# The product that updates the recurrent state, issued as 64x64 tiles instead of 64x128 tiles

## The reference, cut to what matters

```python
def step(state, inp):
    q_i, k_i, v_i, g_i, dec_i, kcd_i = inp
    attn = einsum('bhcd,bhed->bhce', q_i, k_i) * dec_i
    v_new = v_i - einsum('bhcd,bhde->bhce', kcd_i, state)
    out_i = einsum(q_i * exp(g_i), state) + einsum(attn, v_new)
    state = state * exp(g_last) + einsum('bhcd,bhce->bhde', k_i * exp(g_last - g_i), v_new)
```

## Time and profile before

| | |
|---|---|
| runs shown | 2787.59, 2787.88, 2792.42 us, median 2787.88 |
| the profiled execution's own time | 2787.02 us |
| its span | 2785.1 us |
| TensorE (matmul) busy | 2496.7 us, 90% |
| TensorE (weight load) busy | 1718.8 us, 62% |
| VectorE, ScalarE, GpSimd busy | 1660.4, 1492.5, 1802.1 us |
| TensorE's granted clock, mean | 0.982 of full speed |
| L548, the state product | 1792 matmul records, 162.8 us busy |

### The profile page before, as it was taken

One profiled execution on the slowest core, in us unless ns is written; L12 is line 12 of the kernel. 1 busy time (PEld: TensorE's weight loads), 2 busy tenths in 40 slices (PEclk: granted clock), 3 DMA queues, 4 the chain that ended last, 5 costly groups with the idle time before them and its releaser, 6 DMA issues.

```text
span 2785.1 us, 104069 instructions
## 1 busy us (share of the span) xinstructions
PE 2496.7 (90%) x41680; PEld 1718.8 (62%) x41680; DVE 1660.4 (60%) x2967; ACT 1492.5 (54%) x3206; POOL 1802.1 (65%) x1829
## 2 busy tenths in 40 slices
PE   3599999989999998999999899999899999998799
PEld 1366666666666666666666566666666666666444
DVE  5466666666666666666666566666566666665322
ACT  1456566555556566555556566555565566554211
POOL 0576667787666666787666667787666667787100
PEclk8799999999999999999999999999999999998899
DMA  3111011111111011111111011011110111110200
GB/s 96 35 35 31 16 31 39 30 34 33 35 35 31 17 30 40 28 35 33 35 35 31 17 31 39 28 35 33 36 35 16 32 31 39 27 35 2 58 22 16
DMA packets 71100, 90.28 MB, mean 32 GB/s; under 512 B 16720, under 2 KB 39376, under 8 KB 70480
## 3 DMA queue, kind: packets, MB, share of 16 engines
q1 hardware_dynamic: 70608, 83.40, 11.7%
HBM read 78.30 MB, written 5.08 MB: 30 GB/s over the span
## 4 chain that ended last, share of the span: by engine, by line
PE 68%; DVE 20%; issue 6%; DVEq 1%; ACT 1%; DMA 0%; POOLq 0%; ACTq 0%; SPq 0%; POOL 0%
PE ps_two L406 9%; PE ps_two L582 8%; DVE XW L926 6%; PE ps_p L422 5%; PE ps_p L524 4%; PE ps_state L387 4%; PE ps_two L387 4%; PE ps_state L548 4%; DVE XW L937 4%; PE ps_p L419 3%; PE ps_p L418 3%; PE ps_p L502 3%; PE ps_two L572 3%; DVE hT L990 2%; PE ps_p L532 2%
## 5 line engine op out<-in xcount | busy, mean ns | idle before, releaser
L1072 POOL TENSOR_TENSOR Sd<-St,el 128x512 f32<-128x512 f32 x192 | 201.2, 1048 | 605.3 <-DVEq L971 500.1
L1108 POOL TENSOR_SCALAR hT<-idx_s,lutb 128x134 f32<-128x134 int32 x480 | 355.4, 744 | 27.5
L954 DVE TENSOR_SCALAR Vn<-ps_p,bR 128x128 f32<-128x128 f32 x512 | 164.6, 349 | 257.2 <-PE ps_p L497 183.6
L742 ACT ACTIVATE Xs<-XW 64x512 f32<-64x512 f32 x320 | 200.9, 628 | 207.7 <-DVE XW L937 201.5
L418 PEld LDWEIGHTS ps_p<-XW,U 64*64 64x64 f32 x5120 | 170.9, 137 | 222.3 <-issue 222.3
L857 DVE SCALAR_TENSOR_TENSOR cacc<-ps_two,cw,cacc 128x1022 f32<-128x1022 f32 (+2 forms) x192 | 243.1, 1266 | 84.2 <-ACT cacc L653 81.8
L418 PE MATMUL ps_p<-XW,U 64*64 64x64 f32 x5120 | 189.3, 223 | 112.0 <-DVE XW L926 104.2
L387 PE MATMUL ps_two<-xnT,w_qkv 128*128 128x512 f32 x512 | 258.7, 629 | 21.6 <-DVEq L862 19.8
L857 DVE SCALAR_TENSOR_TENSOR cacc<-ps_state,cw,cacc 128x1022 f32<-128x1022 f32 (+2 forms) x192 | 244.4, 1273 | 39.7 <-ACT cacc L653 18.2
L387 PE MATMUL ps_state<-xnT,w_qkv 128*128 128x512 f32 x512 | 253.3, 618 | 0.8 <-DVEq L862 0.8
L422 PEld LDWEIGHTS ps_p<-XW,P 64*64 64x64 f32 x5120 | 166.7, 136 | 132.1 <-issue 132.0
(11 more groups left out here) (156 smaller groups left out, 6115.5 us busy)
## 6 DMA issues: line engine op xcount, KB each, us to landing
qg<-g_scratch SPq DMA_DIRECT2D x64, 512.0 KB, 7.3
g_st<-g_scratch SPq DMA_DIRECT2D x64, 256.0 KB, 5.5
w_qkv<-in_wqkvz SPq DMA_DIRECT2D x16, 512.0 KB, 3.8
w_z<-in_wqkvz SPq DMA_DIRECT2D x16, 256.0 KB, 3.1
w_o<-in_wout SPq DMA_DIRECT2D x16, 256.0 KB, 2.8
idx_s<-in_idx SPq DMA_DIRECT2D x32, 67.0 KB, 1.9
fw_scratch<-looked_up SPq DMA_DIRECT2D x32, 67.0 KB, 1.9
Kg<-in_x SPq DMA_DIRECT2D x2, 1024.0 KB, 7.6
```

The lines of the kernel that those rows point to most:

```text
L742: act.activation(Xs[(1 - a) * C:(2 - a) * C], X[a * C:(a + 1) * C, 1], ACT.Copy).then_inc(s["x_c"], 1)
L1072: pool.tensor_tensor(Sd[:, :, :, :], St[:, c % 2, :, :, :], el[:, R.par, :, :, c].unsqueeze(3).broadcast_to([P, BB, RATIO, P]), ALU.mult). ...
L1108: m = pool.tensor_scalar(slots[k], idx_s[:, :], float(k), lutb[:, k:k + 1], ALU.is_equal, ALU.mult)
```

## The change

Each 64x128 product is cut into two 64x64 products, over the two halves of the key columns. A half of the columns is a half of the output partitions, so the four tiles of one b (two value heads, two halves) take the four 64x64 positions of the array. A `sem_inc` instruction goes ahead of each b's tiles and now carries the wait for `Vn`.

```diff
                         for b in range(BB):
                             wait_read(pe, R, "vn", c * BB + b)
+                            pe.sem_inc(s["tiled"], 1)
                             for a in range(RATIO):
                                 r = slice(a * C, (a + 1) * C)
 
-                                m = pe.matmul(ps[6 + a][:, b * P:(b + 1) * P], Kd[r, b, c, :], Vn[r, cur, b, :],
-                                              start=True, stop=True)
+                                for half in (slice(0, C), slice(C, P)):
+                                    m = pe.matmul(ps[6 + a][half, b * P:(b + 1) * P], Kd[r, b, c, half], Vn[r, cur, b, :],
+                                                  start=True, stop=True)
                         m.then_inc(s_filled, 1)
```

## The result

The changed kernel takes 2785.12 us (median of 14 runs, 2780.31 to 2791.43) against 2789.51 us for the kernel before (14 runs): ratio 0.9984, interval 0.9977 to 0.9992. It is faster by 4.4 us. The forecast was 14.7 us (2772.5). The sign was right and the size wrong by a factor of three; the measured time lies just inside the upper end of the range, and above the 2782.3 from which on the prediction itself would not have called a run faster.

The account below looks back on a forecast made before the run. The bound was taken to be the loop in which TensorE and VectorE hand the state to and fro. Chunks 0, 1, 2, 3, 5: 0.045 - 0.05 + 0.045 + 0.21 + 0.21 = 0.46 us a round, 32 rounds 14.7 us: 2772.5, range 2765 to 2786.

Parts of the forecast that it names:

- The array time of the tiles: State product: four passes of four 64x64 tiles stream the same 128 columns, so array time stays at four passes of 0.11.
- L502 0.21 earlier, kept in the chunks 3 and 5: L502 shares the state product's new tile shape and streams 0.21 us earlier; all of it counts in chunks 3 and 5.
- Rival B: Chunks 3 and 5: the 0.21 is not kept, something else is late behind it; 2785.7 us, chance 0.06.
- The slack: Chunk 3: the state was ready at 959.91, L524 starts at 960.38; 0.42 us of slack, so all of the 0.21 counts.
- Nothing in the chunks 4 and 6: VectorE's state update L969 waits there for `gated`, not for the state product; no gain, and the sem_inc costs nothing.
- L550's end, 0.045 in the chunks 0 and 2: State product (L548 before) ends 0.045 us earlier through a shorter first load; gained in each of chunks 0 and 2.
- The `sem_inc` in chunk 1: State product waits for Vn: 0.06 later by the sem_inc, 0.05 earlier by the load; loss 0.02 to 0.08, taken as 0.05.
- rivals A and C: A: b = 1's sem_inc holds loads back, 2788, chance 0.08. C: sem_inc waits until the array drains, 2825, chance 0.05.
- L497's row: Chunk 0: L497's eight records with a sem_inc in the middle take 0.65 us, so the sem_inc was priced at nothing.
- L502's 0.21 is gained in the chunks 1, 2, 4 and 6 too, but there TensorE only waits longer for the state.: Recurrence: the 0.21 us was counted as no gain in these chunks, and the longer wait at no cost.
- the range's lower end: Whole kernel: chunk 1 without loss and 0.05 more in each of chunks 3 and 5 gives 2765 us.
- Rival D, the rule on loads: State product: four loads in the same pass can't hide, three more of 0.05 a chunk; 2798.5 us, chance 0.03.

Follow-up runs that it names:

- e1: Changed kernel with three idle-time matmuls and one sem_inc on TensorE in chunk 1, ahead of the state product: 2772.95 us, ratio 0.9943.
- e8: Changed kernel with one idle-time matmul and a sem_inc behind chunks 4 and 6, none in chunk 1: 2785.25 us, ratio 0.9979.
- e4: Kernel before with only the two sem_inc a chunk, tiles still 64x128: 2796.38 us, ratio 1.0030.
- e7: Kernel before with a 128x256 memset on VectorE ahead of Vn in chunk 1: 2798.83 us, ratio 1.0032.
- e5: Changed kernel with the fourth gate projection moved from ahead of the recurrence into chunk 1: 2725.81 us, ratio 0.9772.
- e6: Kernel before with the fourth gate projection moved from ahead of the recurrence into chunk 1: 2752.78 us, ratio 0.9858.

## Why the prediction was wrong

By its own steps:

- **The array time of the tiles: right.** Four tiles a pass keep 0.11; sixteen records take 0.67 (forecast 0.665).
- **L502 0.21 earlier, kept in the chunks 3 and 5: right to 0.003.** The periods fall by 0.207 and 0.208. Rival B is out. The slack was enough.
- **Nothing in the chunks 4 and 6: right.** The period of 4 to 5 is 2.66 before and after, and Vn of chunk 7 starts 1.94 behind chunk 6's state product in both; L971 follows `gated`.
- **L550's end, 0.045 in the chunks 0 and 2: 0.03.** The end comes 0.048 earlier by the records, but VectorE starts 0.02 later behind it (0.156 instead of 0.135 in chunk 2; chunk 0 the same 0.02), so 0.027 is left in each.
- **The `sem_inc` in chunk 1: 0.09 instead of 0.06.** L550 starts 0.146 behind Vn's first half, L548 before 0.055. b = 1 is not held back anywhere: rivals A and C are out, as L497's row said. The chunks 0 and 1 together lose 0.03 (forecast 0.005). The sum of an ordinary round is 0.41 instead of 0.46.
- **The failed step is a sentence ahead of the rivals: "L502's 0.21 is gained in the chunks 1, 2, 4 and 6 too, but there TensorE only waits longer for the state."** The idle time was priced at nothing. In chunk 1 it is 0.27 longer (0.21 by the earlier L502 of chunk 0, 0.09 by the `sem_inc`, less 0.03 by which Vn itself comes earlier), and behind it the clock falls in 11 rounds where it fell in 2. Eleven falls instead of two take back 10.7 us in the profiled executions; filling the stretch (e1) gives back 12.2 us of the median and leaves no fall. That the stretch has to be idle for the falls is shown, by e1 and its control e8. That its being 0.27 longer is what raised their number is argued: e4's lower clock speaks for it, e7's other five runs against it. No rival had the clock.
- The sum was made against an execution of 2787.0 us with two falls, and the median of the 14 runs is 2789.5; against that median the same 14.7 us would be 2774.8.
- Two slips that change nothing: the range's lower end was worked out as 0.05 and twice 0.05 us a round more, which is 2787.0 - 19.5 = 2767.5, not 2765; and in chunk 7 the load comes 0.36 behind the start of L532's last matmul, not 0.30.
- That the clock falls at all could have been read before. The page's row of clocks is too coarse: a slice is 70 us, a fall 3.4. But a second round of the kernel before, beside that of the earlier trace rows, shows it. This is its state product in the chunks 1 to 4:

```profile
1661.33 0.75 PE L548 MATMUL ps_state<-Vn,Kd 64*128 64x128 f32 x8 [1.36 <-DVE Vn L954]
1664.40 1.23 PE L548 MATMUL ps_state<-Vn,Kd 64*128 64x128 f32 x8
1667.64 0.71 PE L548 MATMUL ps_state<-Vn,Kd 64*128 64x128 f32 x8
1670.49 0.72 PE L548 MATMUL ps_state<-Vn,Kd 64*128 64x128 f32 x8
```

  Eight records in 1.23 us instead of 0.71, and a period of 3.24 for chunk 2 to 3 instead of 2.46. A kernel that already loses the clock behind a wait is one in which a longer wait can't be priced at nothing before its clock has been read; how many more falls there would be could not be read from it.
- Rival D, the rule on loads: four tiles keep 0.11 a pass in the changed kernel too, with each pass loading the rows in flight, so the trace again doesn't agree with what the Trainium skill, "TensorE: Matmul & The Clock Gate", Part 3, The mechanism, says of row groups in its list. The same section also lets a load run ahead into a background weight buffer; no run here shows whether that is what happens.

## What to carry to other kernels

Where TensorE waits, a faster matmul turns into idle time, and idle time can cost the clock: read the granted clock of the stretches behind the longest waits, in several rounds of the loop, before pricing the wait at nothing. And compare the mean clock of all runs, not only the one profile: here that one was typical for the changed kernel and not for e7. The remedy is to put independent work of the same size into the wait, useful work first (64 us here, with the tiles, most of it because the work no longer stands on the path), filler where there is none (12 us, and 10 in the last round). A wait moved from a matmul to an instruction of its own costs only where the engine really waits.

## What the runs showed of the hardware that was not expected

- The clock falls behind idle stretches as short as 1.36 to 1.63 us amid small matmuls: 2, 5, 9 and 11 falls in 32 rounds of one execution each, at 1.36, 1.45, 1.61 and 1.63 us, and none at 0.07 or 0.34. The number differs from run to run, and in which rounds they come stays open: in the changed kernel the idle stretch is 1.63 us in a round with a fall and in a round without.
- In the recurrences the clock stays at half for 3.4 us, sometimes 6.8 (e5 and e6), and 3.4 cost 1.2 to 1.4 us where TensorE and VectorE pass the state to and fro, 6.8 in chunk 0 3.1 to 3.2.
- VectorE's wait for a product ends about 0.02 us later after a pass of four tiles than after a pass of two, by the modelled ends (0.156 instead of 0.135 in chunk 2).
- A `sem_inc` on TensorE's queue that finds its condition met costs nothing between 128-column passes (e4: the periods of the chunks 2 to 6 are unchanged to 0.002 us); one that really waits lets the next load start 0.09 us later than a wait on the load itself.
